# Attention's row-maximum scores spread evenly over the rounds and started a third of a head pair earlier

## What is computed

```
x = x + attn(layernorm(x), Wqkv, bqkv, Wo, bo)      # x: 2 x 1024 x 512, 16 heads of 32
scores = k q / sqrt(32), causal;  attn = softmax(scores);  out = attn v
```

## Time and profile before

| | us |
|---|---|
| median of 3 runs | 2069.95 (2061.15 to 2071.49) |
| the profiled execution's own time | 2079.13 |
| its span, first to last instruction | 2077.3 |
| mean granted TensorE clock over the span | 0.939 |
| from the turn for pair 0 to that for pair 15 | 185.03 to 543.42 |

### The profile page before, as it was taken

The page is one execution under the profiler, slowest core; times in us unless marked ns, Lnnn a source line. Parts: engine busy times, 40 slices in busy tenths (PEclk is TensorE's granted clock), DMA queues, the critical chain, the costliest instruction groups (busy, mean ns, idle before and its releaser), DMA issues. The chain is left out here.

```text
span 2077.3 us, 24075 instructions
## 1 busy us (share of the span) xinstructions
PE 1822.1 (88%) x7553; PEld 1284.7 (62%) x7553; DVE 993.3 (48%) x2218; ACT 609.8 (29%) x1184; POOL 482.3 (23%) x790
## 2 busy tenths in 40 slices
PE   6996999998898999999689999978878788878886
PEld 5884444444476877878567677755556555655554
DVE  5435767676551232322485677783333333333332
ACT  3121555554521122121232422202323222222222
POOL 2003333335610000000242411112222222222222
PEclk9996999999999999999889999988999899999998
DMA  6235567665309000000200111138787788778784
GB/s 238 105 140 135 151 167 190 175 169 156 106 18 334 0 1 1 1 0 1 99 1 1 62 44 44 41 116 271 249 283 246 251 264 261 263 257 267 233 288 128
DMA packets 129323, 298.91 MB, mean 144 GB/s; under 512 B 23952, under 2 KB 34704, under 8 KB 128976
## 3 DMA queue, kind: packets, MB, share of 16 engines
q1 hardware_dynamic: 114896, 262.11, 36.9%
q0 software_dynamic: 14336, 35.66, 8.5%
HBM read 232.66 MB, written 60.46 MB: 141 GB/s over the span
## 5 line engine op out<-in xcount | busy, mean ns | idle before, releaser
L799 ACT ACTIVATE probs<-bank 128x512 f32<-128x512 f32 (+3 forms) x384 | 169.1, 497 | 196.4 <-PE bank L740 190.9
L1748 POOL DMA_INDIRECT out_x<-e_y,row_out x64 | 100.9, 1576 | 488.4 <-ACT e_y L1806 469.8
L1784 PE MATMUL bank<-w_gate,xgt 128*128 128x352 f32 x512 | 211.9, 570 | 0.0
L1852 DVE TENSOR_TENSOR e_hidden<-e_silu,bank 128x352 f32<-128x352 f32 x64 | 33.4, 521 | 273.3 <-issue 222.4
L1784 PE MATMUL bank<-w_up,xgt 128*128 128x352 f32 x512 | 162.4, 460 | 0.0
L724 PE MATMUL bank<-k_stack,q_stack 96*128 96x512 f32 (+3 forms) x384 | 142.8, 400 | 20.2 <-DMA k_stack<-qk_parts 10.4
L740 PE MATMUL bank<-q_stack,k_stack 98*128 98x512 f32 (+3 forms) x384 | 142.4, 399 | 19.7 <-DMA q_stack<-neg_max_t 12.0
L1784 PEld LDWEIGHTS bank<-w_gate,xgt 128*128 128x128 f32 x512 | 119.2, 245 | 62.6 <-issue 38.2
L222 PE MATMUL bank<-ln_xt_hi,gu_hi 128*128 128x512 f32 x352 | 141.3, 401 | 14.4 <-DMA gu_lo<-fp_out 9.7
L1764 PE MATMUL bank<-ident,xg 128*128 128x128 f32 x256 | 51.2, 331 | 116.5 <-DMA xg<-expert_rows,row_in 115.6
L754 PE MATMUL bank<-probs,v_ones 128*64 128x512 f32 (+3 forms) x768 | 148.4, 524 | 0.0
(11 more groups left out here) (233 smaller groups left out, 3800.9 us busy)
## 6 DMA issues: line engine op xcount, KB each, us to landing
w_gate<-in_w_gate SPq DMA_DIRECT2D x64, 704.0 KB, 5.6
w_up<-in_w_up SPq DMA_DIRECT2D x64, 704.0 KB, 7.6
w_down<-in_w_down SPq DMA_DIRECT2D x64, 512.0 KB, 8.0
q_stack<-qk_parts SPq DMA_DIRECT2D x96, 128.0 KB, 3.1
k_stack<-qk_parts SPq DMA_DIRECT2D x96, 128.0 KB, 3.5
w_down<-in_w_down SPq DMA_DIRECT2D x64, 192.0 KB, 8.7
fp_words<-in_fp_words SPq DMA_DIRECT2D x32, 264.0 KB, 3.2
fp_out<-fp_hi SPq DMA_DIRECT2D x32, 264.0 KB, 2.2
```

The costliest lines, as they stand in the source:

```text
L799: act.activation(probs[u % PROBS][:, 0:cols], m.bank[EXPB[u % 3]][:, 0:cols], ACT.Exp, scale=scale).then_inc(exp_ready, 1)
L1748: pool.indirect_dma_start(out=a["out"][:, :], out_offset=bass.IndirectOffsetOnAxis(ap=row_out[u][:, :], axis=0), in_=y[u % 2][:, :], in_of ...
L1784: last = pe.matmul(m.bank[bank[u % 2]][:, 0:F], xt[u % 2][:, k, :], w[u][:, k, :], start=(k == 0), stop=(k == KT - 1))
```

## The change

The maxima become one stream over the whole loop. The function `maxima_of(p)` lists what belongs to pair p: the units 8 to 23 of pair p + 1, then the units 0 to 7 of pair p + 2, with the turn for pair p + 1 put in front of the 19th unit, so 25 entries that PE spreads over the 24 `exp_unit`: six or seven a round. The eight units 0 to 7 of pair 1 are computed ahead of pair 0. The turn's output goes into the ring of three banks like a unit's, and one semaphore, `max_bank_read`, counts the reads of all entries. Entry `at` waits for `at - 2` reads, which again allows three ahead.

DVE follows the same list, and its unpacking work gets new places: `vector_bits` of slice 2p after entry 2, `vector_lo` of slice 2p - 1 after entry 6, `vector_bits` of slice 2p + 1 after entry 10, `vector_lo` of slice 2p after entry 20, `invert` after entry 22. No operation is added or removed, and SP's order stays as it was.

```diff
-    EXP_ROUND, MAX_ROUND = U // ROUNDS, U // (ROUNDS - 1)
+    EXP_ROUND = U // ROUNDS
+    LEAD, TURN_AT = 8, 18
+
+    def maxima_of(p):
+
+        first = [] if p >= 0 else [("unit", 0, n) for n in range(U)] + [("turn", 0)] + [("unit", 1, n) for n in range(LEAD)]
+        for n in range(U if p >= 0 else 0):
+            if n == TURN_AT and p + 1 < PAIRS:
+                first.append(("turn", p + 1))
+            q, i = divmod(U * (p + 1) + n + LEAD, U)
+            if q < PAIRS:
+                first.append(("unit", q, i))
+        return first
...
@@ PE
+            maxima(maxima_of(-1))
             pe.wait_ge(ones_set, 2 * SLOTS + 4)
-            for n in range(U):
-                max_unit(0, n)
-            turn_max(0)
             for p in range(PAIRS):
+                ahead = maxima_of(p)
                 for r in range(ROUNDS):
-                    ahead = MAX_ROUND if r < ROUNDS - 1 and p + 1 < PAIRS else 0
-                    scored_ahead = 0
-                    for n in range(EXP_ROUND):
-                        exp_unit(p, EXP_ROUND * r + n)
-                        while scored_ahead < ahead * (n + 1) // EXP_ROUND:
-                            max_unit(p + 1, MAX_ROUND * r + scored_ahead)
-                            scored_ahead += 1
-                        if r == ROUNDS - 1 and n == 2 and p + 1 < PAIRS:
-                            turn_max(p + 1)
+                    for n in range(EXP_ROUND * r, EXP_ROUND * (r + 1)):
+                        exp_unit(p, n)
+                        maxima(ahead[len(ahead) * n // U:len(ahead) * (n + 1) // U])
@@ DVE
             for p in range(PAIRS):
-                for r in range(ROUNDS - 1):
-                    for n in range(MAX_ROUND):
-                        if p + 1 < PAIRS:
-                            max_part(p + 1, MAX_ROUND * r + n)
-                        if n == 4 and r == 0:
-                            dq.vector_bits(dve, 2 * p)
-                        if n == 4 and r == 1 and p >= 1:
-                            dq.vector_lo(dve, 2 * p - 1)
-                        if n == 4 and r == 2:
-                            dq.vector_bits(dve, 2 * p + 1)
-                if p + 1 < PAIRS:
-                    join_max(p + 1)
-                if p >= 1:
-                    invert(p - 1)
-                if p + 1 < PAIRS:
-                    copy_max(p + 1)
-                dq.vector_lo(dve, 2 * p)
+                ahead = maxima_of(p)
+                for n in range(U):
+                    maxima(ahead[len(ahead) * n // U:len(ahead) * (n + 1) // U])
+                    if n == 2:
+                        dq.vector_bits(dve, 2 * p)
+                    if n == 6 and p >= 1:
+                        dq.vector_lo(dve, 2 * p - 1)
+                    if n == 10:
+                        dq.vector_bits(dve, 2 * p + 1)
+                    if n == 20:
+                        dq.vector_lo(dve, 2 * p)
+                    if n == 22 and p >= 1:
+                        invert(p - 1)
```

More of the change, by code:

```diff
@@ L518, in attention_phase @@
     ROUNDS = 4
-    EXP_ROUND, MAX_ROUND = U // ROUNDS, U // (ROUNDS - 1)
+    EXP_ROUND = U // ROUNDS
[9 more added lines that the diff above has]
+        return first
+    place = {entry: i for i, entry in enumerate(entry for p in range(-1, PAIRS) for entry in maxima_of(p))}
     FIRST_DONE = 2 * TPC
@@ L590, in place_max @@
                 slot = p % SLOTS
-                sp.wait_ge(max_copied, p + 1)
+                sp.wait_ge(max_bank_read, place["turn", p] + 1)
                 for j in range(2):
@@ L717, in max_unit, with maxima @@
                 q, half, cols = MAX_UNITS[i]
-                u, slot = U * p + n, p % SLOTS
+                at, slot = place["unit", p, n], p % SLOTS
                 if n == 0:
                     pe.wait_ge(stack_loaded[slot], 192 * (p // SLOTS + 1))
[L721 to L724, removed]
+                need(pe, max_bank_read, at - 2)
+                pe.matmul(m.bank[MAXB[at % 3]][:, 0:cols], qs[slot][j][0:ROWS, q * P:(q + 1) * P],
                           ks[slot][j][0:ROWS, half * CH:half * CH + cols], start=True, stop=True).then_inc(max_scored, 1)
             def turn_max(p):
+                at = place["turn", p]
                 pe.wait_ge(neg_ready, p + 1)
-                pe.matmul(m.bank[MAXB[0]][0:4 * QT, 0:P], top[:, :, :, :].rearrange("p j a q -> p (j a q)"), m.ident[:, :],
+                need(pe, max_bank_read, at - 2)
+                pe.matmul(m.bank[MAXB[at % 3]][0:4 * QT, 0:P], top[:, :, :, :].rearrange("p j a q -> p (j a q)"), m.ident[:, :],
                           start=True, stop=True).then_inc(max_turned, 1)
+            def maxima(entries):
+                for kind, *which in entries:
+                    if kind == "unit":
+                        max_unit(*which)
+                    else:
+                        turn_max(*which)
             def exp_unit(p, n):
@@ L836, in max_part @@
                 q, half, cols = MAX_UNITS[i]
[L837 to L838 removed]
+                at = place["unit", p, n]
+                bank, part = m.bank[MAXB[at % 3]], parts[p % 2][:, j, half, q:q + 1]
+                dve.wait_ge(max_scored, U * p + n + 1)
                 if (q + 1) * P - half * CH == cols:
[L840 to L841 removed]
+                    need(dve, max_bank_read, at - 3)
+                    dve.tensor_tensor_reduce(out=masked[at % 4][:, 0:cols], in0=bank[:, 0:cols], in1=wide_mask[:, CH - cols:],
                                              scale=1.0, scalar=-3e38, op0=ALU.add, op1=ALU.max,
[L843 to L846 removed]
+                                             accum_out=part).then_inc(max_bank_read, 1)
+                else:
+                    dve.tensor_reduce(part, bank[:, 0:cols], AX.X, ALU.max).then_inc(max_bank_read, 1)
             def join_max(p):
                 both = parts[p % 2]
[L850 removed]
+                dve.wait_ge(max_bank_read, place["unit", p, U - 1] + 1)
                 dve.tensor_tensor(both[:, :, 0, TPC:], both[:, :, 0, TPC:], both[:, :, 1, TPC:], ALU.max).then_inc(max_joined, 1)
@@ L862, in copy_max, with maxima @@
                     dve.wait_ge(max_placed[(p - 2) % SLOTS], 64 * ((p - 2) // SLOTS + 1))
-                dve.tensor_copy(top_t[p % 2][:, :], m.bank[MAXB[0]][0:4 * QT, 0:P]).then_inc(max_copied, 1)
+                dve.tensor_copy(top_t[p % 2][:, :], m.bank[MAXB[place["turn", p] % 3]][0:4 * QT, 0:P]).then_inc(max_bank_read, 1)
+            def maxima(entries):
+                for kind, *which in entries:
+                    if kind == "turn":
+                        copy_max(*which)
+                    else:
+                        max_part(*which)
+                        if which[1] == U - 1:
+                            join_max(which[0])
             def invert(p):
```

14 lines of the change are left out of this document (2 added, 12 removed).

## The result

The changed kernel takes **2099.7 us** (median of 4 runs, 2098.51 to 2102.5) against 2070.72 of the kernel before on the same chip: a ratio of 1.0151, interval 1.0117 to 1.0184, 29 us slower. The forecast was 2093, with 2062 to 2112 as its range.

A forecast was written before the change was run, and what follows sets the result against it. Bound by a loop: turn, SP's queue, DMA landing, DVE's unpacking, last maxima, turn. Eleven periods +32.8 and the others -9.5 give +23.3 on 2079.1, so 2102; that execution lies 9.2 above the median, hence 2093, range 2062 to 2112.

The forecast's parts named there:

- The landing: Scales of slice 2p + 1 land as late as before, 17.5 to 19.8 us after the turn, mean 18.5.
- DVE's wait: DVE reads entry 10 near 11.5 us after the turn, then stands about 7 us for the slice's scales.
- From the landing to the turn: Unpacking, five remaining reads and the values up to the turn: 7.6 us with PE's clock low, 5.7 without.
- The drop: PE's clock falls to 1.2 GHz nearly every period, 2 to 4 us after its idle stretch before entry 14 starts.
- B: The moment the scales of slice 2p + 1 land; PE resumes at B + 1.4, the turn comes at B + 7.6.
- the upper bound of 8.4: Landing to turn if all of that stretch runs at the low clock: 8.4 us.
- Eleven periods: The eleven like periods between turns, each 18.5 + 7.6: 287.1 us against 254.3 before, +32.8.
- The others: Pair 0, the periods before and behind the eleven, and the tail: together -9.5 us.
- the join meets POOL: Rival: POOL's normalizing holds DVE's join, five periods grow by 2.2 us; 2104 or 2114 us, chance 0.14.
- The sum: Eleven periods +32.8 and the remaining parts -9.5: net +23.3 us.
- The even stream pays: Rival: slice there at entry 10, so PE sets a period of 20.3 us; about 2030 us, chance 0.06.
- The slice is late, but the clock is kinder: Rival: PE's clock stays up or returns quickly, period 24.2 us; about 2072 us, chance 0.17.

The follow-up runs named there:

- e9: Changed kernel with thirteen spare matmuls that no engine reads, put before entry 14 where PE idles: 2091.9 us, ratio 1.0123 to the kernel before.
- e4: Changed kernel with SP issuing the load of slice 2p + 1 ahead of the twelve stack loads: 2062.5 us, ratio 0.9952 to the kernel before.
- e1: Changed kernel with the unpacking (vector_bits) of slice 2p + 1 after entry 17 instead of entry 10: 2063.4 us, ratio 0.9969 to the kernel before.
- e7: e1 with POOL's normalizing moved behind the scaling of slice 2p + 1: 2046.7 us, ratio 0.9871 to the kernel before.
- after_again: The changed kernel timed once more, unaltered, as reference on the chip of e9: 2108.7 us, ratio 1.0182 to the kernel before.
- e10: Kernel before, without the even stream, with unpacking behind copy_max, normalizing late, one bias addition a pair: 2062.0 us, ratio 0.9961 to the kernel before.

## Why the prediction was right

The direction and the mechanism held, and the size within 7 us; the numbers step by step:

- **The landing.** Taken as 18.5 after the turn over the eleven periods. Measured 17.5 to 19.7, mean 18.4. It did not move with the change, as argued from the queue of SP: the issue stayed at 14.2.
- **DVE's wait.** Entry 10 was to be read near 11.5, with about 7 us of standing. DVE came there near 14, and its wait is 4.2 on average (45.9 in 11), so that the 5 to 8 us of the forecast were reached in one period only. I had taken over the 4.7 from the turn to `exp_unit` 0, though two more `exp_unit` and six `max_unit` now lie between: it is 6.0 (310.70 to 316.71). That is 1.3 of DVE's 2.5; for the rest it read entry 10 later behind PE than I had taken. By about the same 1.3 PE came late to entry 14, at 16.9 instead of 15.5, and so idled 2.8 (30.6 in 11) instead of 4.4. The landing and PE's resuming at landing + 1.5 do not depend on this, but the clock does, as the next point shows.
- **From the landing to the turn.** Predicted 7.6, measured 7.1 to 8.7, mean 8.2. The term is off by 0.6 in each period. Without a drop I had 5.7, and e9 measured 6.0. The drop was to come "nearly every time, 2 to 4 us after its start, so it holds until about B + 6.7". It came every time, and 1.6 to 3.8 after the start of the idle stretch. But that start is 1.4 later than I had put it, so the low stretch is, too: where it lasts 6.8 us, in eight periods, it ends between B + 7.3 and B + 8.9, covers most or all of the round of values (4.11 above) and makes the term 8.5, close to the upper bound of 8.4. In the other three the clock is low for only half as long, and the term is 7.3. So the step that was mis-sized is PE's arrival at entry 14, by way of the 4.7 above.
- **Eleven periods.** Predicted 287.1, measured 291.9.
- **The others.** Predicted -9.5, measured -7.4. Pair 0 with its longer lead -1.8 (said -1.6), the period before the eleven -1.0 (-1.5), the second to last -4.1 (-2.8), and the last only -0.8, where I had said -4.

That last one is a step that failed. "That to 543.42 (27.00) has no stack loads, so no new wait: 23" left out POOL. In the changed kernel, DVE and POOL at the last join:

```profile
569.72 1.18 POOL L479 TENSOR_TENSOR fp_scaled<-fp_bits,fp_scales 128x528 f32<-128x528 f16 x1
570.12 0.80 DVE L867 TENSOR_TENSOR max_parts<-max_parts 128x8 f32<-128x8 f32 x1
570.86 5.11 POOL L725 TENSOR_TENSOR x_residual<-x_residual,bo_rows 128x512 f32<-128x512 f32 x4
571.03 1.12 DVE L870 TENSOR_SCALAR neg_max<-max_parts 128x16 fp32r<-128x16 f32 x1
572.18 1.19 DVE L872 SCALAR_TENSOR_TENSOR neg_max<-max_parts,neg_max 128x16 fp32r<-128x16 f32 x1
573.42 0.63 PE L745 MATMUL bank<-ident,neg_max 128*32 128x128 f32 x2 [4.64 <-DVE neg_max L872]
```

The join's three operations, 0.17, 0.17 and 0.30 in the other pairs, take 3.1 and hold the turn. This is the mechanism of my rival "the join meets POOL", at a place that I had not looked at. Where I had put it, in the eleven periods, it did not happen: the join ended at 333.73 and the normalizing began at 334.15, 0.4 later, where my working had 0.3.

**The sum** was +23.3 and is +30.2 in the traces up to the output projection: the miss of 6.9 is 4.8 in the eleven and 2.1 in the others. The medians say +29.0. The forecast of 2093 is 7 below the result. That the two spans differ by 23.4, almost as forecast, is chance: the untouched program was 6.9 shorter in the profile after. The others come out well in part by luck, too: -4.1 for -2.8 in the second to last period makes up for some of the -0.8 for -4 in the last.

**The rivals.** *The even stream pays* named the landing as its condition; e4 and e1 met the condition in two ways and gained 36 to 37 us, and e7 has periods of 20.9 where I had 20.3. Its time of 2030 was not reached, 2042.6 being the best. *The slice is late, but the clock is kinder* was worked out at 24.2 a period, and e9 measured 24.36 when spare matmuls kept the clock up; the kernel as it is gives PE no such help. For the clock, the forecast's own difference between 5.7 and 7.6 was 1.9 a period, and 1.7 to 2.2 were measured. By the rule of the Trainium skill (TensorE: Matmul & The Clock Gate, "HAM oscillation — how this bites in real kernels"), 6.7 us at the low level would cost 3.35, an estimate. The eight periods with the long low stretch measure less, 8.5 against the 6.0 of e9. That the loss is smaller fits DVE's pace for part of that stretch, which the rule does not count; that reason was argued and not tested.

## What to carry to other kernels

Close the loop from one event to its own next occurrence before you price an edit: if a transfer's landing stands in it, time saved elsewhere gives nothing, and any instruction moved ahead of the landing takes the whole queue of its engine with it. Where the producer is only a few buffers ahead, count where it stops and what its idle time does to its clock afterwards. And after each cure look for what the freed engine now runs into: here the same small DVE operation met POOL in one place after another.

## What the runs showed of the hardware

- In the changed kernel PE idles 2.15 to 4.36 us in each of the eleven periods, and in each the clock fell to its 1.2 GHz level. It fell 1.6 to 3.8 us after the idle stretch began, and so not at one place relative to PE's work: at 358.0 PE was still idle (it resumed at 358.95), at 412.6 it had been running since 411.20. Spare matmuls in the gap, which do no useful work and left idle stretches of at most 0.64 us there, kept the clock at 1.00 and made the eleven periods 19.0 us shorter (e9 against after_again).
- Small DVE operations beside a POOL tensor operation end with it or shortly after it in the rows below. The join's L870 has one tensor source of 128x16 and ran from 571.03 to 572.15; POOL's first bias addition, a quarter of 5.11, ran from 570.86 to 572.14. In e1 `vector_lo` ended 0.56 after the normalizing, a little less than its usual length of 0.70. The unpacking's first operation is held too. In e10:

```profile
376.91 1.28 POOL L706 TENSOR_TENSOR x_residual<-x_residual,bo_rows 128x512 f32<-128x512 f32 x1
...
377.45 2.50 DVE L468 TENSOR_SCALAR fp_spread<-fp_words,fp_shift 128x528 int32<-128x528 int32 x1
...
378.15 1.51 POOL L670 TENSOR_SCALAR_AFFINE_SELECT probs<-probs 128x128 f32<-128x128 f32 x6
```

  It takes 0.49 elsewhere; here it went on through the bias addition and to 0.3 after the last masking. Masking alone does not always hold it: in the changed kernel it took 0.49 at 318.90, beside three maskings from 318.40 to 319.54. The Trainium skill (GPSIMD Engine Reference, 1. Specifications) has the two engines share their SBUF interfaces, and contention for VectorE instructions that read two SBUF inputs or run in a two-port mode. `vector_lo` reads two, and its 0.70 to 1.96 agrees. L870 and L468 have one tensor source; that they were held too, 0.17 to 1.12 and 0.49 to 2.50, agrees only if they ran in such a mode, which no row shows. DVE's reads of PSUM kept their usual time: in e1 the masked reads of 256 columns at 320.78 and 321.13 took 0.42 each while the normalizing ran.
